# Soft-expert stage of a vision tower: three PSUM buffers for the gate products, second products in closed groups of six, and four image buffers

## The reference, cut to what matters

```python
logits = jnp.einsum('bnd,esd->bnes', x, phi)
dispatch = jax.nn.softmax(logits, axis=1)
combine = jax.nn.softmax(logits.reshape(B, N, E * S), axis=-1).reshape(B, N, E, S)
slots = jnp.einsum('bnd,bnes->besd', x, dispatch)
h = jax.nn.gelu(jnp.einsum('besd,edh->besh', slots, w1) + b1[None, :, None, :])
y = jnp.einsum('besh,ehd->besd', h, w2) + b2[None, :, None, :]
out = jnp.einsum('besd,bnes->bnd', y, combine)
```

## Time and profile before

| What | us |
|---|---|
| three timed runs | 1216.7, 1220.22, 1220.92 (median 1220.22) |
| the profiled execution | 1217.52 |
| its span, first to last instruction | 1215.7 |
| TensorE busy in the span | 1070.5 (88%) |
| ScalarE busy | 693.3 (57%) |
| VectorE busy | 414.5 (34%) |

### The profile page before, as it was taken

How to read it: one execution, slowest core, us unless ns; L and a number is a source line. 1 busy time by engine, 2 the same in 40 slices (tenths; PEclk the granted TensorE clock), 3 DMA queues, 4 the chain that set the end, 5 groups by cost and what they waited for, 6 DMA issues and landing times. The chain is left out here.

```text
span 1215.7 us, 22327 instructions
## 1 busy us (share of the span) xinstructions
PE 1070.5 (88%) x7440; PEld 703.3 (58%) x7440; DVE 414.5 (34%) x1096; ACT 693.3 (57%) x1389; POOL 250.4 (21%) x270
## 2 busy tenths in 40 slices
PE   8799978997899999999989999876249999999993
PEld 7378645663234444444444445445239999999992
DVE  3186696874001110101010101576762222222220
ACT  0276695766888888878878885255004334334331
POOL 0152031000000000000000000020165555555532
PEclk9898987997999999989999999889559999999997
DMA  9100002885554454444544441101349999999995
GB/s 302 34 1 1 1 1 106 263 343 211 113 121 107 112 120 109 108 102 110 121 109 105 105 120 38 44 1 33 93 156 321 312 309 307 312 309 307 305 290 86
DMA packets 72354, 183.75 MB, mean 151 GB/s; under 512 B 15626, under 2 KB 30314, under 8 KB 71952
## 3 DMA queue, kind: packets, MB, share of 16 engines
q1 hardware_dynamic: 59200, 166.22, 45.4%
q0 software_dynamic: 12640, 16.16, 6.9%
q10 hardware_dynamic: 432, 0.26, 0.1%
HBM read 147.50 MB, written 36.67 MB: 151 GB/s over the span
## 5 line engine op out<-in xcount | busy, mean ns | idle before, releaser
L1011 ACT ACTIVATE sle_H<-sle_hp 128x1024 f32<-128x1024 f32 x384 | 370.3, 1023 | 88.5 <-PE sle_hp L953 88.4
L953 PE MATMUL sle_hp<-keep_G,keep_dT 99*128 99x512 bf16 (+1 forms) x1024 | 210.3, 335 | 31.0 <-ACT sle_H L1011 17.9
L1425 ACT ACTIVATE ext_H<-ext_hp,ext_bias 128x128 f32<-128x128 f32 x378 | 104.3, 375 | 171.7 <-issue 157.1
L967 PE MATMUL sle_up<-sle_H,sle_cw 128*32 128x384 f32 x2048 | 195.0, 499 | 0.2 <-ACT sle_H L1011 0.2
L953 PEld LDWEIGHTS sle_hp<-keep_G,keep_dT 99*128 99x128 bf16 x1024 | 83.8, 99 | 179.1 <-issue 65.4
L1030 DVE STREAM_TRANSPOSE sle_UT<-sle_up 128x384 f32<-128x384 f32 x64 | 37.1, 583 | 394.4 <-PE sle_up L967 392.6
L1383 PE MATMUL ext_yp<-ext_w,ext_H 128*128 128x192 f32 x756 | 139.7, 335 | 0.6 <-issue 0.6
L938 POOL COPY sle_cw<-keep_CT 128x128 f32 (+1 forms) x64 | 18.7, 293 | 529.5 <-PE sle_up L967 431.7
L1383 PEld LDWEIGHTS ext_yp<-ext_w,ext_H 128*128 128x128 f32 x756 | 121.1, 190 | 8.4 <-issue 0.9
L967 PEld LDWEIGHTS sle_up<-sle_H,sle_cw 128*32 128x32 f32 x2048 | 53.9, 110 | 92.8 <-issue 91.9
L1368 PE MATMUL ext_hp<-ext_xT,ext_w 128*128 128x128 f32 x756 | 96.0, 277 | 0.0
(11 more groups left out here) (244 smaller groups left out, 1217.6 us busy)
## 6 DMA issues: line engine op xcount, KB each, us to landing
ext_w<-W SPq DMA_DIRECT2D x126, 576.0 KB, 5.4
pieces<-hid_gp SPq DMA_DIRECT2D x16, 1152.0 KB, 5.1
keep_G<-pieces SPq DMA_DIRECT2D x64, 288.0 KB, 3.8
keep_G<-pieces SPq DMA_DIRECT2D x64, 192.0 KB, 3.7
pieces<-hid_gp SPq DMA_DIRECT2D x8, 768.0 KB, 4.3
keep_dT<-pieces SPq DMA_DIRECT2D x64, 96.0 KB, 2.7
keep_G<-pieces SPq DMA_DIRECT2D x64, 96.0 KB, 3.5
keep_dT<-pieces SPq DMA_DIRECT2D x64, 64.0 KB, 3.6
```

Source lines behind the costliest of these rows:

```text
L953: mm = pe.matmul(hp[k % 2][:, j, off:off + width], dT[:, p, c * P:(c + 1) * P], G[:, p, (c // 2) * HID + at:(c // 2) * HID + at + width], ...
L967: mm = pe.matmul(up[32 * e:32 * e + 32, half, 0:HALF], cw[:, p, 2 * e + grp, :], H[:, p, at:at + HALF], start=(p == 0 and grp == 0), stop= ...
L1011: act.activation(H[:, p, WIDTH * k:WIDTH * (k + 1)], hp[k % 2][:].rearrange("p a c -> p (a c)"), ACT.Gelu_apprx_tanh).then_inc(gelu_done, 1)
L1425: act.activation(H[:, q, c, :], hp[q][:, c % 2, (c // 2) * P:(c // 2 + 1) * P], ACT.Gelu, bias=bias[:, q, c:c + 1]).then_inc(gelu_done, 1)
```

## The change

It has four parts, all in this stage.

- `hp` gets a third tile of two banks, so a gate product waits for the gelu three before it. With `up` that makes eight banks; `yps` moves into the free end of the second bank of `up`. To make room there, the mixing products are cut at column 512 in place of 384: 512 columns in bank 0, 256 in bank 1.
- Since `yps` shares a bank with `up`, the second products run in closed groups: six blocks in each odd image, behind its first gate product, in a time when no mixing group is open. VectorE adds each group to `acc` (`gather`) in place of one addition per tile. The mixing of the new pair in bank 1 waits for that (`y_left`).
- The mixing calls move. In an even image those of image n-1 stand behind gate products 0 and 3; in an odd one behind 2 and 4. The two banks are written in the order 1, 0 by the odd image of a pair, and VectorE transposes bank 1 (256 columns) and then bank 0 (512 columns).
- `G` and `dT` have four buffers. Image n is loaded when image n-4 has its six gate products; images 2 and 3 as soon as the pieces are in DRAM. The two new buffers get their bias rows by two more DMAs and their ones by two fills on GpSimd, ahead of its first copy.

Cut to its core:

```diff
-def load_image(sp, g, pieces, n, p):
+def load_image(sp, pieces, n, G, dT, arrived):
...
-        sp.dma_start(g.dT[rows, p, :], same).then_inc(g.image_in[p], 16)
+        sp.dma_start(dT[rows, :], same).then_inc(arrived, 16)
         each = pieces[tokens, 0:copies, 0:SLOT_E * HID]
-        sp.dma_start(g.G[rows, p, :], each).then_inc(g.image_in[p], 16)
+        sp.dma_start(G[rows, :], each).then_inc(arrived, 16)
...
-            pool.memset(g.dT[PROWS:BROWS], 1.0).then_inc(g.ones, 1)
+            for i, dT in enumerate(g.dT):
+                pool.memset(dT[PROWS:BROWS, :], 1.0).then_inc(g.ones, 1)
+                pool.wait_ge(g.ones, i + 1)
...
-    OPS, WIDTH, BANKS = 6, 1024, 2
+def slot_experts(nc, g, CT, zn, pieces, b_dram):
+
+    OPS, WIDTH, BANKS, DEEP = 6, 1024, 2, 3
+    CUT = 512
+    PART = HID // 32 // (TILE_IMAGES // 2)
...
-        hp = [s.ps(f"hp{i}", [P, BANKS, 512]) for i in range(2)]
+        G = [*g.G, *(s.sb(f"G{i}", [BROWS, SLOT_E * HID], BF16) for i in range(2, 4))]
+        dT = [*g.dT, *(s.sb(f"dT{i}", [BROWS, ALL_SLOTS], BF16) for i in range(2, 4))]
+        more_ones, more_rows = s.sem("more_ones"), s.sem("more_rows")
+        hp = [s.ps(f"hp{i}", [P, BANKS, 512]) for i in range(DEEP)]
         up = s.ps("up", [P, 2, 512])
-        yps = s.ps("yps", [P, 512])
-        cw_zero, cw_ready, hid_ready, gelu_done, mix_done, ut_done, y_ready, y_done, turn, step, h_done = (
-            s.sem(n) for n in ("cw_zero", "cw_ready", "hid_ready", "gelu_done", "mix_done", "ut_done", "y_ready", "y_done", "turn",
-                               "step", "h_done"))
+        U = ((up[:, 0, 0:CUT], 0, CUT), (up[:, 1, 0:HID - CUT], CUT, HID - CUT))
+        yps = up[:, 1, HID - CUT:HID - CUT + D]
...
+            for i in range(2, 4):
+                sp.dma_start(G[i][PROWS:BROWS, :], b_dram).then_inc(more_rows, 16)
 
             def image(n, m, r, first):
                 if first and m < 2:
                     return
-                sp.wait_ge(hid_ready, OPS * (n - 1))
-                load_image(sp, g, pieces, n, m % 2)
+                if not (first and m < 4):
+                    sp.wait_ge(hid_ready, OPS * (n - 3))
+                load_image(sp, pieces, n, G[m % 4], dT[m % 4], g.image_in[m % 4])
...
             pool.wait_ge(cw_zero, 1)
+            for k in range(2):
+                pool.wait_ge(g.g_out[k], TILE_STORED * TILES // 2)
+            for i in range(2, 4):
+                pool.memset(dT[i][PROWS:BROWS, :], 1.0).then_inc(more_ones, 1)
+                pool.wait_ge(more_ones, i - 1)
...
-            def hidden(n, p, k, start):
-                if not (start and k < 2):
-                    pe.wait_ge(gelu_done, OPS * n + k - 1)
+            def hidden(n, b, k, start):
+                if not (start and k < DEEP):
+                    pe.wait_ge(gelu_done, OPS * n + k + 1 - DEEP)
                 for j, off, c, at, width in parts(k):
-                    mm = pe.matmul(hp[k % 2][:, j, off:off + width], dT[:, p, c * P:(c + 1) * P],
-                                   G[:, p, (c // 2) * HID + at:(c // 2) * HID + at + width], start=True, stop=True)
+                    mm = pe.matmul(hp[k % DEEP][:, j, off:off + width], dT[b][:, c * P:(c + 1) * P],
+                                   G[b][:, (c // 2) * HID + at:(c // 2) * HID + at + width], start=True, stop=True)
                 mm.then_inc(hid_ready, 1)
 
-            def mix(n, p, grp, pair, first_pair):
+            def mix(n, p, grp, pair, first_pair, drained):
 
                 pe.wait_ge(gelu_done, OPS * n + 3 * grp + 3)
                 if grp == 0:
                     pe.wait_ge(cw_ready, n + 1)
-                for half in range(2):
+                for bank in (range(2) if p == 0 else (1, 0)):
                     if p == 0 and grp == 0 and not first_pair:
-                        pe.wait_ge(ut_done, 2 * pair - 1 + half)
+                        pe.wait_ge(ut_done[bank], pair)
+                        if bank == 1 and drained is not None:
+                            pe.wait_ge(y_left, drained)
+                    to, at, width = U[bank]
                     for e in range(SLOT_E):
-                        at = (4 * grp + e) * HID + half * HALF
-                        mm = pe.matmul(up[32 * e:32 * e + 32, half, 0:HALF], cw[:, p, 2 * e + grp, :], H[:, p, at:at + HALF],
+                        h = (4 * grp + e) * HID + at
+                        mm = pe.matmul(to[32 * e:32 * e + 32], cw[:, p, 2 * e + grp, :], H[:, p, h:h + width],
                                        start=(p == 0 and grp == 0), stop=(p == 1 and grp == 1))
                     mm.then_inc(mix_done, 1)
 
-            def down(tile, par, blocks):
-
-                if blocks[0] == 0:
-                    pe.wait_ge(ut_done, 8 * tile + 8)
-                    if not isinstance(tile, int) or tile > 0:
-                        pe.wait_ge(y_done, tile)
+            def down(par, pairs, blocks):
+
+                for bank in range(2):
+                    pe.wait_ge(ut_done[bank], pairs)
                 for b in blocks:
-                    mm = pe.matmul(yps[:, 0:D], UT[:, par, b, :], g.w2[:, b, :], start=(b == 0), stop=(b == BLOCKS - 1))
-                if blocks[-1] == BLOCKS - 1:
-                    mm.then_inc(y_ready, 1)
+                    mm = pe.matmul(yps, UT[:, par, b, :], g.w2[:, b, :], start=(b == blocks[0]), stop=(b == blocks[-1]))
+                mm.then_inc(y_ready, 1)
 
             def image(n, m, r, first):
                 p = m % 2
                 start = first and m == 0
-                j = m % TILE_IMAGES
-                if start:
-                    pe.wait_ge(g.image_in[0], 16 * IMAGE_LOADS)
-                else:
-                    pe.wait_ge(g.image_in[p], 16 * IMAGE_LOADS * (BODY // 2 * r + m // 2 + 1))
+                j = m % TILE_IMAGES // 2
+                pair = BODY // 2 * r + m // 2
+                drains = not (first and m < TILE_IMAGES)
+                drained = pair - TILE_IMAGES // 2 + 1 if drains else None
+                if first and m == 2:
+                    pe.wait_ge(more_rows, 32)
+                    pe.wait_ge(more_ones, 2)
+                pe.wait_ge(g.image_in[m % 4], 16 * IMAGE_LOADS * (BODY // 4 * r + m // 4 + 1))
                 for k in range(OPS):
-                    hidden(n, p, k, start)
-                    if k % 2 == 1 and k < 4 and not start:
-                        mix(n - 1, 1 - p, k // 2, BODY // 2 * r + (m - 1) // 2, first and m <= 2)
-                if 1 <= j <= 6 and not (first and m < TILE_IMAGES):
-                    down(2 * r + m // TILE_IMAGES - 1, (m // TILE_IMAGES - 1) % 2, range(4 * (j - 1), 4 * j))
+                    hidden(n, m % 4, k, start)
+                    if p == 0 and k in (0, 3) and not start:
+                        mix(n - 1, 1, k // 3, None, False, None)
+                    if p == 1 and k == 0 and drains:
+                        down((m // TILE_IMAGES - 1) % 2, pair, range(PART * j, PART * (j + 1)))
+                    if p == 1 and k in (2, 4):
+                        mix(n - 1, 0, k // 4, pair, first and m == 1, drained)
 
             program(pe, image)
 
             for grp in range(2):
-                mix(IMAGES - 1, 1, grp, IMAGES // 2 - 1, False)
-            down(TILES - 1, (TILES - 1) % 2, range(BLOCKS))
+                mix(IMAGES - 1, 1, grp, None, False, None)
+            down((TILES - 1) % 2, IMAGES // 2, range(BLOCKS))
...
-                    act.activation(H[:, p, WIDTH * k:WIDTH * (k + 1)], hp[k % 2][:].rearrange("p a c -> p (a c)"),
+                    act.activation(H[:, p, WIDTH * k:WIDTH * (k + 1)], hp[k % DEEP][:].rearrange("p a c -> p (a c)"),
...
+            def leave(par, j, pair):
+
+                for bank, count in ((1, 8 * pair + 7), (0, 8 * pair + 8)):
+                    dve.wait_ge(mix_done, count)
+                    src, at, width = U[bank]
+                    dve.transpose(UT[:, par, at // 32:(at + width) // 32, 32 * j:32 * j + 32],
+                                  src.rearrange("p (b c) -> p b c", c=32)).then_inc(ut_done[bank], 1)
+
+            def gather(t, j, count):
+
+                dve.wait_ge(y_ready, count)
                 ht = g.h[:, bass.ds(t, 1), :].rearrange("p o d -> p (o d)")
+                dve.tensor_tensor(acc[:], yps, ht if j == 0 else acc[:], ALU.add).then_inc(y_left, 1)
+                dve.wait_ge(y_left, count)
...
+                j = m % TILE_IMAGES // 2
+                pair = BODY // 2 * r + m // 2
+                tile = 2 * r + m // TILE_IMAGES
                 if m % 2 == 0:
+                    if not (first and m == 0):
+                        leave((m // TILE_IMAGES if j else m // TILE_IMAGES - 1) % 2, (j - 1) % (TILE_IMAGES // 2), pair - 1)
+                elif not (first and m < TILE_IMAGES):
+                    gather(tile - 1, j, pair - TILE_IMAGES // 2 + 1)
+                    if j == TILE_IMAGES // 2 - 1:
```

(48 more changed lines are left out.)

14 lines of the change are left out of this document (8 added, 6 removed).

## The result

The changed kernel takes 1189.42 us (median of four runs, 1186.1 to 1193.73) against 1220.57 for the kernel before (four runs). The ratio is 0.9752, with a 95% interval of 0.9723 to 0.9781: 31 us less between the medians, where 22 were forecast. The profiled execution took 1189.59 us, with a span of 1187.8, which is 27.9 less than the profiled execution of the kernel before.

A forecast was written before the change was run, and what follows sets the result against it. TensorE, nearly full, and the gelu chain on two PSUM buffers were taken as the bounds. 15.3 + 5.0 + 0.8 - 0.2 = 20.9 us less than 1217.5 gave 1196.6, set at 1198 for the runs' median; range 1188 to 1209.

The forecast's parts named there:

- Two regimes with the same price: Images before the change: a full TensorE or the chain product, gelu, product on two PSUM buffers, about 7.0 us either way.
- A full TensorE takes 13.37 us a pair in a later tile, 12.34 in the first: Steady part: no gelu waits in later tiles, two in the first; 15.3 us less net and 5.0 less.
- Mixing cut at nothing: Mixing products cut at 512 and 256: columns set the time, so zero cost; upper bound 31 us.
- Blocks covered by 0.4 us from the transposes: Second products in odd images: VectorE's transposes end 0.4 us before the blocks come, so zero cost.
- The additions: VectorE's three more additions a tile: idle engine, costed at nothing; 12 us if that cover went.
- Loads and fills at the start at nothing: Stage start: GpSimd's fills and copies and image 2's loads finish before TensorE needs them, zero cost.
- Image 0: three stops go, 0.8 less: First image of the stage: three stops of about 0.26 us for the second buffer go, 0.8 us less.
- the slow clock kept as it is: Stage start and behind the first loop turn: TensorE's losses at 1.2 GHz were kept unchanged.
- The stall at the loop turn stays as it is.: Two loop turns: TensorE's stalls of 3.44 and 3.15 us stay, giving 2.6 us of the gain back.
- rival 3: Start and first loop turn: clock rises earlier, 2.1 us saved, 3.0 more if the turn keeps it; chance 0.08.
- gelu waits of the first tile: First tile: five gate products in a row leave gelu waits, charged 2.8 us; the range's low end drops them.

The follow-up runs named there:

- the even order: The changed kernel with mixing calls behind gate products 0 and 3 in odd images too, three products apart everywhere: 1185.62 us, ratio 0.9743.
- the added wait: The changed kernel with one more TensorE wait, for the image's last gelu, ahead of each jump back: 1199.08 us, ratio 0.9876.
- Written out: The changed kernel with its 64 images written out, so that the two jumps back are gone: 1181.75 us, ratio 0.9696.

## Why the prediction was right, and where it was short

The direction, the range (1188 to 1209) and the mechanism of the steady part held; the measured 1189.4 lies near the lower end, and the gain was 31 us where 22 were forecast. Of the 10.8 us that the stretch gained over the forecast's 20.9, 8.7 come from two terms that it kept as they were, the last two below.

- *Two regimes with the same price.* Right. With two buffers and new loads alone the 7.01 us stay; with the third buffer alone taken back, 53 us more were expected and 56 measured.
- *A full TensorE takes 13.37 us a pair in a later tile, 12.34 in the first.* Measured 13.29 and, in the first tile, (334.99 - 298.26) / 3 = 12.24. The 0.08, times 28, are 2.2 us. The six blocks took the forecast 1.95, so it lies in the gate and mixing products with the switches between them, which I took whole from the old order; it wasn't sorted out further. In the first tile the two waits were 0.25 and 0.31 us (at 304.78 and 305.69), not 0.43 and 0.49; the other 0.35 us between this pair and the 11.33 of the even order, where they are gone, the sum doesn't have.
- *Mixing cut at nothing.* Right, by the run with the cut alone.
- *Blocks covered by 0.4 us from the transposes.* 0.46; the 512 columns took 0.72 and not 0.78. The additions stood in no one's way.
- *Loads and fills at the start at nothing.* Right: no wait of TensorE for a load in that stretch. GpSimd's first copies ended at 293.08, 0.9 us ahead of the first mixing call, where 1.8 was forecast; in the run with even order this cover was gone. I missed that the four buffers, worth nothing alone, are worth 42 us given the third gate buffer (1231.87 against 1189.42).
- *"Image 0: three stops go, 0.8 less", and the slow clock kept as it is.* This step failed: 4.6 us less. The first mixing call is at 293.99, takes 1.50 us and not 2.79, and the mean clock of the first 14 us is 0.80 and not 0.54. It is 0.54 to 0.56 in all four kernels with two gate buffers and 0.79 to 0.81 in all seven with three, so it goes with the buffer and is no accident of one execution. At half the rate, 1.2 GHz in place of 2.4, a mean of 0.54 is 12.9 us of the 14 at the lower level and 0.80 is 5.6; the 7.3 us between them are worth some 3.6 us, by this estimate. Which property of the denser start does it was not tried apart. The Trainium skill ("TensorE: Matmul & The Clock Gate", Part 1 on the HAM clock gate) has sustained activity release the throttle; these eleven traces agree so far as in each the clock rose while TensorE was at work.
- *"The stall at the loop turn stays as it is."* This step failed too, by 4.9 us for both turns. I took the stall for a fixed gap after the array's last work. It follows the sequencer's last wait ahead of the jump, which the third buffer brings forward; its idle time fell by 1.6 and 1.0 us. There was also less work at the lower clock. The first mixing call behind the second turn took 1.43 us (607.28 to 608.71) where the kernel before had 2.16 (635.13 to 637.29); behind the first turn it took 2.7 us in both.

The earlier clock at the start is the first part of my rival 3, which had a chance of 0.08. Its second part, that the first loop turn keeps the clock, didn't come; the second turn gained instead. The shorter stall I had nowhere, and rival 3 calls it untouched. I had the rows for it: 4.29 us from the end of gelu 3 to the first product could be read from the kernel before. That 1189.4 still lies in the range is partly luck: its lower end of 1188 allowed for rival 3's clock, which came in part, and for gelu waits of the first tile going away, which stayed, but for no shorter stall.

## What to carry to other kernels

When two engines hand buffers to each other, work out both prices of a round, the full engine and the chain product, consumer, product: equal numbers can hide that both bind, and then neither more even work nor earlier loads alone gives anything. A new buffer changes more than the wait that it removes: here it also let the sequencer reach the jump earlier and let the clock rise earlier at the start. Look at what was just hidden at the old pace (here loads of about 7 us in a gap of 7.7, which the change made 5.5) before the pace changes.

## What the runs showed of the hardware

- A backward jump of TensorE's program took 4.0 to 5.6 us from the last wait satisfied ahead of it to the first product behind it: 4.29 and 4.01 in the kernel before, 4.66 and 4.99 in the changed one, 4.17 and 5.56 with the added wait. It is hidden as far as work queued ahead of it is still running (visible: 3.44 and 3.15, 1.84 and 2.17, 5.23 and 6.62). Written out, the stall is gone.
- The stage began at the slow clock in all eleven kernels; with stops of 0.2 to 0.3 us between runs of gate products the mean of the first 14 us was 0.54 to 0.56, with most of them gone 0.79 to 0.81.
- VectorE's transpose of 256, 384 and 512 columns of fp32 from PSUM took 0.45, 0.58 and 0.72 us; a line through the three has 0.18 us at width nothing.
